# A fused attention and FFN block: phase 2 turns its rows on VectorE and places them through DRAM, gate logits in narrow tiles

## The chip, the cores and the metric

The kernel runs on one core of one Trainium2 chip. The core has TensorE (matrix products, written PE in the rows, its weight loads PEld), VectorE (DVE), ScalarE (ACT), GpSimd (POOL) and SyncE (SP), which issues all DMAs here; they move data between DRAM and the on-chip memories. TensorE writes to the accumulator memory PSUM only. Engines run side by side and wait for one another by semaphores; each takes its instructions in the order in which the program lists them. The metric is the device time of one execution in microseconds (us).

## What is computed

```python
def _L0_attn_ref(x, Wq, Wk, Wv, Wo, Wa, ba):
    q = _elu_plus_one((x @ Wq) ...)          # H = 16 heads of Dh = 64
    k = _elu_plus_one((x @ Wk) ...)
    v = (x @ Wv) ...
    a = jax.nn.sigmoid(x @ Wa + ba + DECAY_BIAS_SHIFT)
    def step(carry, inp):                    # over all tokens of a sequence
        S = at[..., None, None] * S + kt[..., :, None] * vt[..., None, :]
        z = at[..., None] * z + kt
        num = jnp.einsum('bhk,bhkv->bhv', qt, S)
        den = jnp.einsum('bhk,bhk->bh', qt, z) + eps
        return ((S, z), num / den[..., None])
    ...
    return out @ Wo

def _L0_ffn_ref(x, CB, SCB, bias):
    return jnp.einsum('bsk,nk->bsn', x, CB) * (SCB * (1.0 / 127.0)) + bias

x = L0_attn_x                                # (4, 2048, 512), float32
x = x + _L0_attn_ref(_layernorm(x), ...)
x = x + _L0_ffn_ref(_layernorm(x), ...)
```

## The kernel before

The 8192 tokens are cut into NC = 64 chunks of C = 128. The kernel has two phases, each a function per chunk that every engine runs in its own version; `steps` writes the first and last calls out and puts the middle ones, two chunks per turn, into a hardware loop. Products of full precision are made of three passes (`passes`): a number is split into a rounded high part and the rest, and high x high, high x low and low x high are added up in PSUM.

**Phase 1** (`step`, chunks -1 to NC + 1) makes q, k and v of a chunk from the normalised x (`unit`, `q_unit`, L1267), turns k, computes scores, the carried and the within-chunk part of the numerators and the state update, all as 64x64 tiles of the array. Once in two chunks (b == 1) `gate_logits` (L1395) makes the logits of the decay gates of the next two chunks: `wa` is padded to 64 columns, contraction rows are split in halves a, and the two chunks c lie in the output halves. The two halves a land in two PSUM banks, and VectorE adds them (`logit_sums`, L1049 and L1051). ScalarE makes the exponent, VectorE `decays` (L1057 to L1067): a reciprocal, a running product over each half chunk (two scans), and a zero at the head of each half. SyncE stores decays and products with four DMAs (`store_decays`), and when they have landed loads them back spread over partitions (`spread_decays`, `products`). The finished attention rows are turned by 32x32 blocks on VectorE (L1041) and stored as columns in DRAM (`attn_cols`, L415), so that phase 2 can load them already turned.

**Phase 2** (`step2`, chunks 1 to NC) does, for chunk i: TensorE multiplies the attention columns by Wo (`output_product`, 24 products of 128x512, in two halves of 12) into the bank Y. VectorE adds x (`residual`, L926: x1), takes statistics (L928), adds the bias to a copy (L933: x1b), GpSimd makes the reciprocal deviation (L627), VectorE the normalised rows (L941: x1n). TensorE turns these with eight small transposes (L1212, into the bank TF), ScalarE copies the high part (L842), VectorE subtracts (L1176), and TensorE does the FFN product of 12 passes (bank F). VectorE adds x1b (L1188: y) and SyncE stores y. The rows of the chunk after next are loaded by four DMAs for attention columns (`load_attn`, L427) and one for x (`load_x`, L433); their high and low parts are made by ScalarE (L696, `rows_hi`) and VectorE (L918, `rows_lo`).

TensorE's order in phase 2, at step i: first half of the output product of chunk i, the eight transposes of chunk i-1, second half of the output product, FFN product of chunk i-1:

```python
output_product(0, b, inputs_of_transposes)
...
turned = halves_turned([TF[:, a, :] for a in range(2)], j, x1n[1 - b])
...
output_product(1, b)
...
passes(F[1 - b], (fT_hi, fT_lo), (wf_hi, wf_lo), range(KT), KT).then_inc(F_ready, 1)
```

VectorE's order at step i: L1176 of i-1, `rows_lo` of i+1, `residual` of i with its statistics and normalisation, the output add of i-1. SyncE's: four loads and the x load of chunk i+1, the store of y of chunk i-2.

## Time and profile before

| | |
|---|---|
| median of 3 runs | 2018.64 us (2017.58 to 2019.59) |
| the profiled execution | 2018.3 us, of which the span from first to last instruction 2016.5 us |
| PE busy | 1989.3 us, 99% of the span |
| DVE busy | 1619.3 us, 80% |
| ACT busy | 684.3 us, 34% |
| POOL busy | 385.6 us, 19% |
| DMA | 220.62 MB, 109 GB/s in the mean |

Phase 1 ends at about 1430 us, phase 2 takes the rest. A line of a timeline gives start and length in us, the engine, the line of the code, the operation, what it writes <- what it reads, the tile of the array for products (rows*columns), the shape, and how many instructions were merged (x8); in square brackets the idle time before it and what ended that. SPq is the queue of SyncE: the length there is the time that issuing takes, not the transfer. Names are those of the buffers' owners: phase 2 reuses memory of phase 1, so x1 is shown as relu_t, x1b as exp_t, x1n as k, y as xt, and the high and low parts of everything as w_hi and w_lo. The timing of a product's end is modelled, so what counts is the distance from start to start.

### The profile page before, as it was taken

To read this page: it belongs to the slowest core of one execution; us is meant where nothing else is said; L and a number is where in the kernel's file an instruction comes from. 1 tells how busy PE (TensorE), PEld (TensorE's weight loads), DVE (VectorE), ACT (ScalarE), POOL (GpSimd) and SP (SyncE) were. 2 spreads that over 40 slices of the span, in tenths; PEclk is the share of its full clock that TensorE was granted. 3 is DMA by queue.
4 is the path that set the end of the run, shared out by engine and by line. 5 is a ranking of instruction groups with operands and counts; after the bars stand their busy time and mean duration, and the time that the engine had idled before them with its cause. 6 is when DMAs were issued, how large, how long until landed. Compare 5 with 4: busy or idle time off the path is not lost.

```text
span 2016.5 us, 69510 instructions
## 1 busy us (share of the span) xinstructions
PE 1989.3 (99%) x27422; PEld 1718.6 (85%) x27422; DVE 1619.3 (80%) x2918; ACT 684.3 (34%) x1288; POOL 385.6 (19%) x368
## 2 busy tenths in 40 slices
PE   8999999999999999999999999999899999999998
PEld 7888888888888888888888888888677777777776
DVE  8888888888888888888888888888856666566565
ACT  5333433443343344334334434434311111111111
POOL 3211223322222332212233212222100000000000
PEclk9999999999999999999999999999999999999999
DMA  6343434444343444334344433435544433434442
GB/s 211 86 95 95 113 96 106 106 103 94 95 113 96 107 104 104 94 95 113 96 107 105 103 94 95 115 95 121 135 122 125 116 116 122 125 114 117 123 123 81
DMA packets 461860, 220.62 MB, mean 109 GB/s; under 512 B 296832, under 2 KB 412032, under 8 KB 461824
## 3 DMA queue, kind: packets, MB, share of 16 engines
q1 hardware_dynamic: 461824, 220.15, 41.5%
q8 instruction: 22, 0.36, 0.1%
q14 instruction: 14, 0.11, 0.0%
HBM read 168.59 MB, written 51.44 MB: 109 GB/s over the span
## 4 chain that ended last, share of the span: by engine, by line
PE 95%; SPq 2%; issue 1%; DVE 1%; DMA 1%; POOL 0%; ACT 0%; POOLq 0%; DVEq 0%
PE G L1267 51%; PE DS L1224 18%; PE NUM L1224 9%; PE NUM L1336 3%; PE SC L1212 3%; PE SC L1389 3%; PE DS L1368 3%; PE NUM L1350 3%; PE DS L1409 1%; SPq L393 1%; SPq L415 0%; DMA abc<-decay_rows 0%; SPq L460 0%; SPq L469 0%; DMA norm_rows<-moments 0%
## 5 line engine op out<-in xcount | busy, mean ns | idle before, releaser
L1267 PE MATMUL G<-w_hi,xT_hi 128*128 128x512 f32 x1024 | 406.9, 397 | 0.9 <-DVE w_lo L880 0.9
L1267 PE MATMUL G<-w_lo,xT_hi 128*128 128x512 f32 x1024 | 399.6, 390 | 0.0
L1267 PE MATMUL G<-w_hi,xT_lo 128*128 128x512 f32 x1024 | 399.1, 390 | 0.0
L728 ACT ACTIVATE relu_t<-G 128x512 f32<-128x512 f32 x256 | 153.1, 598 | 445.7 <-PE G L1267 443.5
L1267 PE MATMUL G<-xT_hi,w_hi 128*128 128x256 f32 x1024 | 290.0, 283 | 0.0
L1267 PE MATMUL G<-xT_lo,w_hi 128*128 128x256 f32 x1024 | 289.8, 283 | 0.0
L1267 PE MATMUL G<-xT_hi,w_lo 128*128 128x256 f32 x1024 | 289.8, 283 | 0.0
L1267 PEld LDWEIGHTS G<-w_hi,xT_hi 128*128 128x128 f32 x1024 | 192.4, 188 | 41.8 <-DVE xT_lo L873 1.0
L1267 PEld LDWEIGHTS G<-w_hi,xT_lo 128*128 128x128 f32 x1024 | 192.2, 188 | 41.4
L1267 PEld LDWEIGHTS G<-w_lo,xT_hi 128*128 128x128 f32 x1024 | 192.6, 188 | 35.8
L1224 PE MATMUL DS<-w_hi 128*128 128x512 f32 x512 | 207.4, 405 | 2.6 <-DVE w_lo L918 2.3
L1224 PE MATMUL DS<-w_hi,w_lo 128*128 128x512 f32 x512 | 200.3, 391 | 0.0
L1224 PE MATMUL DS<-w_lo,w_hi 128*128 128x512 f32 x512 | 199.1, 389 | 0.0
L1267 PEld LDWEIGHTS G<-xT_hi,w_hi 128*128 128x128 f32 x1024 | 196.3, 192 | 3.3 <-DVE w_lo L880 0.4
L1267 PEld LDWEIGHTS G<-xT_hi,w_lo 128*128 128x128 f32 x1024 | 196.3, 192 | 2.4
L1267 PEld LDWEIGHTS G<-xT_lo,w_hi 128*128 128x128 f32 x1024 | 196.3, 192 | 0.0
L638 POOL TENSOR_TENSOR xT_in<-xT_in,bias_b 128x256 f32<-128x256 f32 x124 | 140.2, 1161 | 293.1 <-DMA bias_b<-norm_rows 293.1
L842 ACT ACTIVATE w_hi<-SC 128x512 fp32r<-128x512 f32 x64 | 38.2, 597 | 452.4 <-PE SC L1212 452.4
L642 POOL TENSOR_TENSOR xT_in<-xT_in,bias_b 128x256 f32<-128x256 f32 x124 | 177.6, 1463 | 2.4
L1074 DVE TENSOR_TENSOR_SCAN D<-abc,eye 128x512 f32<-128x512 f32 x128 | 175.7, 1372 | 1.9 <-DMA abc<-decay_rows 1.9
L623 POOL TENSOR_TENSOR moments<-vareps,minus_half 128x2 f32<-128x2 f32 x32 | 22.5, 702 | 731.8 <-DVE vareps L862 731.8
L1176 DVE TENSOR_TENSOR w_lo<-SC,w_hi 128x512 fp32r<-128x512 f32 x64 | 44.2, 691 | 140.2 <-ACT w_hi L842 140.2
(136 smaller groups left out, 3800.2 us busy)
## 6 DMA issues: line engine op xcount, KB each, us to landing
abc<-decay_rows SPq DMA_DIRECT2D x256, 128.0 KB, 3.0
pbc<-product_rows SPq DMA_DIRECT2D x256, 128.0 KB, 3.1
attn_cols<-attn SPq DMA_DIRECT2D x512, 64.0 KB, 2.2
at_rows<-attn_cols SPq DMA_DIRECT2D x256, 128.0 KB, 2.7
xt<-in_x SPq DMA_DIRECT2D x64, 256.0 KB, 3.1
x_in<-in_x SPq DMA_DIRECT2D x64, 256.0 KB, 3.1
out_rows<-xt SPq DMA_DIRECT2D x64, 256.0 KB, 3.0
xT_in<-in_xT SPq DMA_DIRECT2D x31, 512.0 KB, 4.3
```

Of the source, the lines that this page charges most:

```text
L638: made = pool.tensor_tensor(x4[:, kt, :, :], x4[:, kt, :, :], norm_b[:, 0, :, :], ALU.subtract)
L642: made = pool.tensor_tensor(x4[:, kt, :, :], x4[:, kt, :, :], norm_b[:, 1, :, :], ALU.mult)
L728: act.activation(relu_t[buffer][:, :], bank[:, :], ACT.Relu)
L1074: nc.vector.tensor_tensor_scan(D[:, hs(r), :].rearrange("p h c -> p (h c)"), abc[:, HH * L * r:HH * L * (r + 1)], eye8[:, :, :].rearrange( ...
L1176: nc.vector.tensor_tensor(by_stretch(fT_lo), both_of(TF), by_stretch(fT_hi).bitcast(fp32), ALU.subtract).then_inc(fT_lo_ready, 1)
L1212: turned.append(nc.tensor.transpose(to[a][:, L * j:L * j + L], rows[ps, 128 * j:128 * j + 128], ident[ps, ps]))
L1224: made = nc.tensor.matmul(to, a[:, kt, :], w[:, kt, :], start=(kt == 0 and n == 0), stop=(kt == tiles_k - 1 and n == 2))
L1267: made = nc.tensor.matmul(to, lhs, rhs, start=(n == 0), stop=(n == len(passes) - 1))
L1336: made = nc.tensor.matmul(num_of(a, e, j), qs[ps, GH * r + j, L * a:L * a + L], (S_mid if a else S[o])[ps, GH * r + j, :], start=(j == 0), ...
L1350: made = nc.tensor.matmul(num_of(a, e, j), M[ps, r, 2 * j + e, :], v1[o][ps, HH * r + 2 * j + e, :], start=False, stop=(j == GH - 1))
L1368: made = nc.tensor.matmul(DS[64 * e:64 * e + 64, U * a + E * j:U * a + E * j + E], k[ps, DH * h:DH * h + DH], vw[ps, h, :], start=True, st ...
L1389: made = nc.tensor.matmul(SC[64 * a:64 * a + 64, at:at + L], kT[ps, GH * r + j, ts], qT[ps, GH * r + j, C * (b ^ r) + L * a:C * (b ^ r) + ...
```

## The change

In phase 2 the eight transposes of TensorE go, except for the last chunk. In their place VectorE turns the normalised rows by 32x32 blocks (`x1t`), SyncE stores them with four DMAs into a scratch tensor in DRAM (`x1_cols`) so that the blocks come to lie where a full transposition would put them, and when these have landed loads the result with one DMA into `fT_in`; ScalarE and VectorE split that. The rows of the FFN weights are loaded in the matching order (16 DMAs instead of 4). The FFN product runs two chunks behind the output product instead of one, so TensorE's order at step i is: output product of i, FFN product of i-2. SyncE's order at step i is: stores of turned blocks of i-1, attention loads of i+2, x load of i+1, load of the placed blocks of i-1, store of y of i-3. VectorE's: normalised rows of i-1, their turning, low part of i-2, y of i-3, `rows_lo` of i+1, `residual` of i, the sum with bias of i-1, variance of i.

In phase 1 the gate logits are made with the full 128 contraction rows and 32 columns, in four column tiles, one for each chunk and half chunk, 64 tokens each, so no halves are added; everything behind them is 64 columns wide and not 128, the two scans become one, and the stores become five DMAs and not four. On TensorE the stage moves from ahead of the within-chunk product to behind it. At the seam of the phases some instructions are placed otherwise.

```diff
-        fT_hi, fT_lo = (w[:, 3, 2, :].rearrange("p (j c) -> p j c", c=C) for w in (w_hi, w_lo))
+        fT_hi, fT_lo = ([w[:, 3, 2 + b, :].rearrange("p (j c) -> p j c", c=C) for b in range(2)] for w in (w_hi, w_lo))
+        fT_in = [t.rearrange("p (j c) -> p j c", c=C) for t in pieces(kT, 2)]
+        x1t = pieces(D, 2)
...
-                    sp.dma_start(raw_wf[kt], CBT[128 * kt:128 * kt + 128, :]).then_inc(wf_loaded, 16)
+                    for x in range(4):
+                        at = 128 * x + SQ * kt
+                        sp.dma_start(raw_wf[kt][x:128:4, :], CBT[at:at + SQ, :]).then_inc(wf_loaded, 16)
...
                     for c in range(2):
                         n = chunk_at(i + 1 + c)
-                        sp.dma_start(decay_rows[bass.ds(n, 1), :].rearrange("o (a h t) -> (o h) a t", a=2, h=H),
-                                     aT[L * c:L * c + H, :].rearrange("h (a t) -> h a t", a=2)).then_inc(decay_stored, 16)
-                        sp.dma_start(product_rows[bass.ds(n, 1), :].rearrange("o (h c) -> (o h) c", h=H),
-                                     pT[L * c:L * c + H, :]).then_inc(decay_stored, 16)
-                    sp.wait_ge(decay_stored, p64[1])
+                        for a in range(2):
+                            g = GR * (2 * a + c)
+                            sp.dma_start(product_rows[bass.ds(n, 1), :].rearrange("o (h c) -> (o h) c", h=H)[:, L * a:L * a + L],
+                                         pT[g:g + H, :]).then_inc(decay_stored, 16)
+                    sp.wait_ge(decay_stored, p80[1])
...
+                turning = exists(i - 1) and exists(i)
+                if turning:
+                    sp.wait_ge(x1t_ready, one[-1])
+                    for g in range(4):
+                        q = SQ * g
+                        sp.dma_start(x1_cols[bass.ds(chunk_at(i - 1), 1), :]
+                                     .rearrange("o (f b t) -> (o f) b t", f=SQ, t=C)[:, :, q:q + SQ],
+                                     x1t[1 - b][q:q + SQ, :].rearrange("f (b t) -> f b t", t=SQ)).then_inc(x1t_stored, 16)
+                if exists(i + 2):
+                    sp.wait_ge(rows_loaded, r64[1])
                     for h in range(2):
-                        wait(sp, oT_lo_ready[h], one[-1])
-                    wait(sp, x1_ready, one[-1])
-                    load(chunk_at(i + 1), 1 - b)
-                if exists(i - 2):
-                    wait(sp, y_stored, y16[-3])
-                    wait(sp, y_ready, one[-2])
-                    sp.dma_start(out_rows[bass.ds(before, C), :], y[b]).then_inc(y_stored, 16)
-            steps(sp, step2, 1, NC + 2)
+                        sp.wait_ge(oT_lo_ready[h], one[0])
+                    load_attn(chunk_at(i + 2), b)
+                if exists(i + 1):
+                    sp.wait_ge(xin_loaded, x16[0])
+                    sp.wait_ge(x1_ready, one[-1])
+                    load_x(chunk_at(i + 1), 1 - b)
+                if turning:
+                    sp.wait_ge(x1t_stored, r64[-1])
+                    if isinstance(i, int) and i == 1:
+                        sp.wait_ge(scores_ready, NC + 1)
+                    if exists(i - 2):
+                        wait(sp, fT_loaded, x16[-2])
+                    if exists(i - 3):
+                        wait(sp, fT_lo_ready, one[-3])
+                    sp.dma_start(fT_in[1 - b].rearrange("p j c -> p (j c)"),
+                                 x1_cols[bass.ds(chunk_at(i - 1), 1), :].rearrange("o (p c) -> (o p) c", p=128))\
+                        .then_inc(fT_loaded, 16)
+                if exists(i - 3):
+                    wait(sp, y_stored, y16[-4])
+                    wait(sp, y_ready, counts(sp, i, 1, (-3,))[-3])
+                    sp.dma_start(out_rows[bass.ds(row(sp, i - 3), C), :], y[1 - b]).then_inc(y_stored, 16)
+            steps(sp, step2, 1, NC + 3)
             sp.wait_ge(y_stored, 16 * NC)
...
+                x16 = counts(act, i, 16, (-2,))
                 r64 = counts(act, i, 64, (1,))
-                act.wait_ge(fT_ready, one[-1])
-                act.activation(by_stretch(fT_hi), both_of(TF), ACT.Copy).then_inc(fT_hi_ready, 1)
+                if exists(i - 2):
+                    act.wait_ge(fT_loaded, x16[-2])
+                    if exists(i - 4):
+                        wait(act, F_ready, one[-4])
+                    act.activation(fT_hi[b], fT_in[b], ACT.Copy).then_inc(fT_hi_ready, 1)
...
-                dve.wait_ge(fT_hi_ready, one[-1])
-                nc.vector.tensor_tensor(by_stretch(fT_lo), both_of(TF), by_stretch(fT_hi).bitcast(fp32),
-                                        ALU.subtract).then_inc(fT_lo_ready, 1)
+                y16 = counts(dve, i, 16, (-4,))
+                r64 = counts(dve, i, 64, (-3,))
+                if isinstance(i, int) and i == NC:
+                    residual_normal(NC, x1[1 - b].rearrange("p (x j f) -> p x j f", x=4, f=SQ),
+                                    x1n[1 - b].rearrange("p (j f x) -> p x j f", x=4, f=SQ))
+                elif exists(i - 1):
+                    residual_normal(one[-1], x1[1 - b], x1n[1 - b])
+                if exists(i - 1) and exists(i):
+                    dve.wait_ge(x1n_ready, one[-1])
+                    if exists(i - 3):
+                        wait(dve, x1t_stored, r64[-3])
+                    nc.vector.transpose(x1t[1 - b], x1n[1 - b]).then_inc(x1t_ready, 1)
+                if exists(i - 2) and exists(i - 1):
...
+                if isinstance(i, int) and i == NC:
+                    dve.wait_ge(fT_hi_ready, NC)
+                    nc.vector.tensor_tensor(by_stretch(fT_lo[1 - b]), both_of(TF), by_stretch(fT_hi[1 - b]).bitcast(fp32),
+                                            ALU.subtract).then_inc(fT_lo_ready, 1)
+                if exists(i - 3):
...
-                        for c in range(2):
-                            for a in range(2):
-                                ps = slice(64 * a, 64 * a + 64)
-                                made = nc.tensor.matmul(DS[64 * c:64 * c + 64, U * a + ZC:U * a + 512], wa[ps, kt, :],
-                                                        xT_in[ps, kt, tokens(c)], start=(kt == 0), stop=(kt == KT - 1))
+                        for a in range(2):
+                            for c in range(2):
+                                g, t = GR * (2 * a + c), C * c + L * a
+                                made = nc.tensor.matmul(DS[g:g + GR, ZC:ZC + L], wa[:, kt, :], xT_in[:, kt, t:t + L],
+                                                        start=(kt == 0), stop=(kt == KT - 1))
...
                         pe.wait_ge(oT_lo_ready[h], one[0])
                     wait(pe, x1_ready, one[-2])
-                    if isinstance(i, int) and i == 1:
-                        output_product(0, b)
-                        output_product(1, b, inputs_of_transposes)
+                    for h in range(2):
+                        output_product(h, b)
+                if isinstance(i, int) and i == NC:
+                    pe.wait_ge(M_ready[1], NC)
+                    pe.wait_ge(x1n_ready, NC)
+                    for j in range(KT):
+                        turned = halves_turned([TF[:, a, :] for a in range(2)], j, x1n[1 - b])
+                    turned[1].then_inc(fT_ready, 1)
+                if isinstance(i, int) and i == 2:
+                    pe.wait_ge(wf_lo_ready, KT)
+                if exists(i - 2):
+                    if exists(i - 4):
+                        wait(pe, y_ready, one[-4])
                     else:
-                        output_product(0, b, inputs_of_transposes)
-                else:
-                    inputs_of_transposes()
-                for j in range(KT):
-                    turned = halves_turned([TF[:, a, :] for a in range(2)], j, x1n[1 - b])
-                turned[1].then_inc(fT_ready, 1)
-                if exists(i) and exists(i - 2):
-                    output_product(1, b)
-                if isinstance(i, int) and i == 1:
...
+                    pe.wait_ge(y_ready, NC - 2)
+                    ffn_product(NC, 1 - b)
             steps(pe, step2, 1, NC + 1)
```

## Rows read from the trace of the kernel before

**Rows 1.** The page: the chain that ended last, shares of the span by engine.
```profile
PE 95%; SPq 2%; issue 1%; DVE 1%; DMA 1%; POOL 0%; ACT 0%; POOLq 0%; DVEq 0%
```

**Rows 2.** Windows of phase 1 and phase 2. us, busy of PE, PEld, DVE, ACT, POOL; clock, DMA.
```profile
60.00:1380.00 1320.00, 1316.28 (x22986) 1176.38 (x22988) 1169.59 (x2086) 520.60 (x985) 327.82 (x270) 1.00 0.41 103
1500.00:1960.00 460.00, 460.00 (x2301) 366.43 (x2300) 282.03 (x524) 87.14 (x158) 28.07 (x52) 1.00 0.40 119
```

**Rows 3.** Timeline, one chunk of phase 2: start and duration in us, engine, line, operation.
```profile
1801.04 0.69 DVE L926 TENSOR_TENSOR relu_t<-DS,x_in 128x512 f32<-128x512 f32 x1 [0.34 <-PE DS L1224]
...
1804.11 0.55 DVE L941 TENSOR_SCALAR k<-relu_t,moments,rstd 128x512 f32<-128x512 f32 x1 [0.65 <-POOL rstd L627]
...
1806.05 0.39 PE L1224 MATMUL DS<-w_hi,w_lo 128*128 128x512 f32 x1
...
1806.76 0.19 PEld L1224 LDWEIGHTS DS<-w_hi 128*128 128x128 f32 x1
1806.76 0.50 PE L1224 MATMUL DS<-w_hi 128*128 128x512 f32 x1
...
1806.87 0.60 ACT L842 ACTIVATE w_hi<-SC 128x512 fp32r<-128x512 f32 x1 [6.98 <-PE SC L1212]
...
1807.50 0.69 DVE L1176 TENSOR_TENSOR w_lo<-SC,w_hi 128x512 fp32r<-128x512 f32 x1 [2.24 <-ACT w_hi L842]
...
1808.11 1.28 DVE L918 TENSOR_TENSOR w_lo<-at_rows,w_hi 128x512 fp32r<-128x512 f32 x2
...
1814.84 0.39 PE L1224 MATMUL DS<-w_hi,w_lo 128*128 128x512 f32 x1
```

**Rows 4.** Groups of VectorE: count | busy us, mean ns | idle before.
```profile
L1041 DVE STREAM_TRANSPOSE attn<-num_sb 128x512 f32<-128x512 f32 x128 | 91.1, 711 | 13.4 <-DMA attn_cols<-attn 0.2
...
L1060 DVE RECIPROCAL aT<-one_exp 128x128 f32<-128x128 f32 x32 | 30.5, 953 | 3.6 <-DVE one_exp L1057 0.5
```

**Rows 5.** Timeline of SyncE's DMA queue, phase 2.
```profile
1801.96 2.86 SPq L427 DMA_DIRECT2D at_rows<-attn_cols  x4
1805.02 0.43 SPq L433 DMA_DIRECT2D x_in<-in_x  x1
1805.68 0.36 SPq L592 DMA_DIRECT2D out_rows<-xt  x1
```

**Rows 6.** Timeline of SyncE's DMA queue, phase 1.
```profile
524.22 3.03 SPq L415 DMA_DIRECT2D attn_cols<-attn  x4
527.48 3.07 SPq L469 DMA_DIRECT2D pbc<-product_rows  x4
```

**Rows 7.** DMA issues: count, KB each, median us from issue to landing.
```profile
attn_cols<-attn SPq DMA_DIRECT2D x512, 64.0 KB, 2.2
...
x_in<-in_x SPq DMA_DIRECT2D x64, 256.0 KB, 3.1
```

**Rows 8.** Timeline, start and end of phase 2.
```profile
1475.68 0.69 DVE L926 TENSOR_TENSOR relu_t<-DS,x_in 128x512 f32<-128x512 f32 x1 [0.43 <-PE DS L1224]
...
2003.28 0.69 DVE L926 TENSOR_TENSOR relu_t<-DS,x_in 128x512 f32<-128x512 f32 x1 [1.64 <-PE DS L1224]
...
2010.11 0.62 PE L1224 MATMUL NUM<-w_hi,w_lo 128*128 128x512 f32 x1
```

**Rows 9.** Timeline of TensorE around the gate stage, phase 1.
```profile
537.55 0.71 PE L1212 MATMUL SC<-ident,k 64*128 64x64 f32 x16
538.19 0.27 PE L1336 MATMUL NUM<-S,qs 64*64 64x65 f32 x1
...
541.16 0.70 PE L1368 MATMUL DS<-vw,k 64*64 64x65 f32 x32
541.65 1.08 PE L1409 MATMUL DS<-xT_in,wa 64*64 64x128 f32 x32
542.52 0.67 PE L1350 MATMUL NUM<-v,M 64*64 64x65 f32 x32
```

**Rows 10.** Timeline of VectorE, the first reading of the gate logits.
```profile
544.33 0.28 DVE L1049 TENSOR_SCALAR logits<-DS 128x128 f32<-128x128 f32 x1
```

More of the change, by code:

```diff
@@ L573, in step2 @@
             def step2(i, _, b):
-                one = counts(sp, i, 1, (-2, -1))
-                x16 = counts(sp, i, 16, (0,))
-                r64 = counts(sp, i, 64, (0,))
-                y16 = counts(sp, i, 16, (-3,))
-                before = row(sp, i - 2)
-                if isinstance(i, int) and i == 2:
+                one = counts(sp, i, 1, (-3, -1, 0))
+                x16 = counts(sp, i, 16, (-2, 0))
+                r64 = counts(sp, i, 64, (-1, 1))
+                y16 = counts(sp, i, 16, (-4,))
@@ L894, in _ @@
             x_lo(1, 1, tiles_of(xT_bank(1)))
-            dve.wait_ge(small_loaded, 48)
+            dve.wait_ge(small_loaded, 80)
             nc.vector.tensor_scalar(wa[:, :, 0:H], wa_raw[:, :, :], 1.0, None, ALU.mult).then_inc(wa_ready, 1)
-            for c in range(2):
-                made = nc.vector.tensor_scalar(minus_ba[L * c:L * c + H, :], ba_c[L * c:L * c + H, :], -1.0, -SHIFT,
+            for g in range(0, 128, GR):
+                made = nc.vector.tensor_scalar(minus_ba[g:g + H, :], ba_c[g:g + H, :], -1.0, -SHIFT,
                                                ALU.mult, ALU.add)
@@ L928, in residual, with residual_deviation @@
                 nc.vector.bn_stats(stats2[:, :], x1[b]).then_inc(stats2_ready, 1)
-            def residual_rest(count, b):
+            def residual_deviation(count, biased=None):
                 dve.wait_ge(stats2_ready, count)
-                nc.vector.tensor_tensor(x1b[b], x1[b], bias_b[:, :], ALU.add)
+                if biased is not None:
+                    with_bias(biased)
                 nc.vector.bn_aggr(moments2[:, :], stats2[:, :]).then_inc(moments2_ready, 1)
@@ new lines, in step2 @@
+                if isinstance(i, int) and i == NC:
+                    dve.wait_ge(fT_hi_ready, NC)
+                    nc.vector.tensor_tensor(by_stretch(fT_lo[1 - b]), both_of(TF), by_stretch(fT_hi[1 - b]).bitcast(fp32),
+                                            ALU.subtract).then_inc(fT_lo_ready, 1)
+                if exists(i - 3):
+                    dve.wait_ge(F_ready, one[-3])
+                    dve.wait_ge(x1b_ready, one[-3])
+                    if exists(i - 4):
+                        wait(dve, y_stored, y16[-4])
+                    nc.vector.tensor_tensor(y[1 - b], F[1 - b], x1b[1 - b], ALU.add).then_inc(y_ready, 1)
@@ L1178, in step2 @@
+                if isinstance(i, int) and i == NC:
+                    dve.wait_ge(y_ready, NC - 2)
+                    with_bias(1 - b)
                 if exists(i + 1):
@@ L1181, in step2 @@
                     residual(one[0], x16[0], b)
-                if exists(i):
-                    residual_rest(one[0], b)
-                    residual_normal(one[0], b)
-                dve.wait_ge(F_ready, one[-1])
-                if exists(i - 3):
-                    wait(dve, y_stored, y16[-3])
-                nc.vector.tensor_tensor(y[1 - b], F[1 - b], x1b[1 - b], ALU.add).then_inc(y_ready, 1)
-            steps(dve, step2, 1, NC + 1)
+                    if isinstance(i, int) and i == 1:
+                        dve.wait_ge(bias_loaded, 16)
+                    residual_deviation(one[0], 1 - b)
+                if isinstance(i, int) and i == 1:
+                    ffn_weights_lo()
+            steps(dve, step2, 1, NC + 3)
         @block.tensor
```

147 lines of the change are left out of this document (70 added, 77 removed).

## The prediction

> **What bounds the kernel now.** I read the chain that ended last first: TensorE holds 95% of it [rows 1]. The reader is to see there that only what shortens TensorE's own list, or makes it wait, moves the time. The windows say the same of each stage: TensorE is busy for 1316.3 of 1320 us in phase 1 and for 460.0 of 460 in phase 2, while VectorE has 89% in the first and only 61% in the second [rows 2]. The clock is granted in full in both (1.00, the 2.4 GHz level). Next the timeline of one chunk of phase 2, to see what TensorE's 8.79 us are made of and how long each hand-over takes, then the DMA queue's own timeline, because the change puts a DRAM round trip in the middle of a chain that has none, and last the gate stage in phase 1.
>
> **Phase 2, the floor on TensorE.** From the last product ahead of one group of eight transposes to the same place a chunk later is 1814.84 - 1806.05 = 8.79 us. The step from that product to the first one behind the transposes is 0.71 us, and the next 35 steps take 1814.84 - 1806.76 = 8.08, so 0.231 each [rows 3]. The transposes thus cost 0.71 - 0.23 = 0.48 us a chunk. The change moves them to VectorE (only the last chunk keeps them). A chunk of TensorE's work becomes 36 x 0.231 = 8.31 us. If nothing else became late, 60 chunks would give 60 x 0.48 = 29 us. This is the gain that the change is after.
>
> **Phase 2, what is late next.** VectorE's work hides easily: it is 61% busy, and the new transposition costs 0.71 us if it is like that of the attention rows [rows 4], so it would stand at about 70%. What matters is the order on three queues that run strictly in order. Follow a chunk i from the start of its residual add, S(i).
> - VectorE and GpSimd: the normalised rows begin 1804.11 - 1801.04 = 3.07 after S(i) [rows 3]; the new step sits where VectorE waits for nothing in between, so this holds. They take 0.55, a tenth goes by to the dependent transposition, which takes 0.71. Turned blocks at S + 4.43.
> - SyncE starts a transfer 0.23 after the VectorE instruction that it waited for (1801.04 + 0.69 = 1801.73, the first load of the next rows is issued at 1801.96) [rows 3, 5]. First store at S + 4.66.
> - Now SyncE issues, in this order: four stores of turned blocks, four loads of attention columns, one load of x, and only then the load of the placed blocks. Four stores of the same shape (32 partitions, 512 runs of 128 bytes) occupy the queue for 527.48 - 524.22 = 3.26 [rows 6]. Four column loads take 1805.02 - 1801.96 = 3.06, the x load with the waits behind it 1805.68 - 1805.02 = 0.66 [rows 5]. For five more waits on semaphores that are already there I add 0.2. Sum 7.18: the load is issued at S + 11.84. The stores have landed by then (the last is issued at S + 7.1, median 2.2 to landing [rows 7]), so that wait is free.
> - The load is 256 KB in 2 KB runs like that of x, 3.1 to landing [rows 7]. S + 14.94.
> - ScalarE starts on it about 0.06 later; VectorE's subtraction starts 1807.50 - 1806.87 = 0.63 after ScalarE's copy [rows 3]. S + 15.63.
> - Behind this subtraction VectorE has, in order, the output add of an older chunk, two subtractions for attention rows, and the residual add of chunk i+2. Steps on that engine are 1808.11 - 1807.50 = 0.61 [rows 3], four of them with a few hundredths for waits 2.5. So S(i+2) = S(i) + 18.1.
>
> This is a ring that closes every two chunks: 18.1 / 2 = **9.05 us a chunk**, against 8.79 now and a floor of 8.31 on TensorE. The queue of SyncE itself needs 3.26 + 3.06 + 0.66 and about 1.4 for the placed load, the output store and the loop, 8.4 a chunk: below 9.05, but over TensorE's 8.31, so even a faster ring would not reach the floor. The products that wait for the subtraction (ready at S + 16.3) then let TensorE stand for about 0.75 us a chunk, perhaps 1.5 in every other one.
>
> Sixty chunks (residual adds at 1475.68 and 2003.28, 527.6 us, 8.79 each [rows 8]) become 30 x 18.1 = 543: **+15.4 us**. Bounds of the ring, from the same rows: transposition at 0.55 as the other 512-column instruction that reads one operand, queue steps at their shortest (0.72 instead of 0.79 and 0.76): 18.1 - 0.16 - 0.4 = 17.5, and a chunk is 8.75; landings half a microsecond later because the DMA engines, now 40% busy [rows 2], carry 512 KB more a chunk in part as 128-byte runs: 18.7, and a chunk is 9.35. I take the middle, since every term is a row of nearly the same instruction.
>
> The Trainium skill's page "VectorE: DVE Perf Modes", section "Rules for kernel authors", says to transpose 128x128 on TensorE where PSUM will do as the destination. By that rule the change goes the wrong way; by the floor alone it would be worth 29 us, by the ring it costs 15. No run so far shows which.
>
> **Start and end of phase 2.** At the start the residual add of chunk 1 no longer waits behind the FFN weights (four steps of 0.61, now a chunk later) and the first FFN product comes two chunks behind; following the queues as above brings the residual add of chunk 3 about 1 us earlier than 1475.68. **-1 us**, bounds -4 and +3. At the end the last residual add is now followed by 2016.5 - 2003.28 = 13.2 us. After the change chunk 62's placed blocks land at S(62) + 14.9, and S(63) is 8.4 to 9.1 behind S(62), so its product can start only at about S(63) + 7.5. Two FFN products of 12 steps stand behind it (5.5), then 0.4, the add 0.69 and the store 3.1: 17.2, **+4 us**. TensorE idles for over 3 us there; in the trace of before TensorE also idles between its last products, and the product at 2010.11 lasts 0.62 instead of 0.39 [rows 3, 8], which is the 1.2 GHz level. If all 24 run so, add 24 x 0.2 = 5. I take +6.
>
> **Phase 1, gate logits.** Once in two chunks, 31 times with this cost. Now 542.52 - 541.65 = 0.87 us for 32 pass records, in groups of four abreast: 8 groups x 0.109 [rows 9]. Each streams 128 columns; after the change 64, over 128 rows and 32 columns of the array. The stage before it streams 65 columns in 8 groups of four in 541.65 - 541.16 = 0.49, 0.06 each. If four tiles still run abreast: 8 x 0.06 = 0.47, a gain of 0.40. But the stage now stands between 64x64 tiles and the full array, one change of tiling more. Price: from the first transposes to the first product of the next tiling 538.19 - 537.55 = 0.64 go by [rows 9], of which eight steps of 0.06 are 0.48; the 0.16 left holds the start of a tiling and the change to the next. I take 0.14. Net 0.26 x 31 = **-8 us**.
> VectorE loses one of two instructions of 0.28 and half of a reciprocal of 0.95 [rows 4, 10], with the scan and the exponent about 1 us per pair. It is off the path by now, so this is worth nothing directly; it makes SyncE's decay stores earlier by as much, which pays for the fifth store (0.45). The logits are read at 544.33 [rows 10], and TensorE would deliver them at about 543 although the stage moved behind the within-chunk product (541.65 + 0.67 + 0.14 + 0.47 = 542.9): covered by over 1 us. Behind that read VectorE has the state update, which covers itself the same way.
>
> **Sum.** Profiled execution 2018.3 (span 2016.5; the median of the runs is 2018.6, the same within 0.02%). 2018.3 - 8 + 15.4 - 1 + 6 = 2030.7. I forecast **2031 us**.
>
> **The rivals.**
> - *The round trip fits* (faster). One mechanism: the load of placed blocks starts and lands so much sooner that the ring closes in less than twice 8.79. For it: 7.2 us of the ring are only issue time, and SyncE has idle time in phase 2 now. Against it: nothing in the issue order lets the load pass the nine transfers ahead of it. It decides below a ring of 17.6. Equality of the whole, with the other terms, lies at 17.7. At TensorE's floor: 2018.3 - 8 - 29 - 1 + 4 = **1984**; at SyncE's 8.4, **1990**. Chance 0.17 for anything faster by over 0.2% (a ring under 17.55).
> - *A draw*: a ring of 17.55 to 17.8, **2018**. 0.13.
> - *The gate tiles do not run four abreast.* Before has groups of four only with two row and two column halves; four column tiles need all rows for each. Two abreast makes 16 groups of 0.058, 0.93 us, dearer than now: 31 x 0.47 = 15 more than forecast, **2045**, 0.13. One at a time 32 x 0.058 = 1.86: **2074**, 0.03. The Trainium skill's page "TensorE: Matmul & The Clock Gate", Part 3, "The mechanism", holds that a weight load overlaps a running matmul only where the row group differs; by it the four would block one another. Against it: in the full array products step at 0.231 although a weight load lasts 0.19 and 512 columns at 2.4 GHz take 0.213 [rows 3], so there a load runs beside a product of the same rows; that is why I give it little.
> - *The ring is longer*: the fuller DMA queue lets loads land later. Landings 0.6 later make a ring of 18.7, 30 x 0.6 = 18 more, **2049**. 0.09.
> - Forecast (a ring of 17.8 to 18.5, four abreast) 0.45.
>
> A change within 0.2% (4 us) is what a measurement of this kernel can tell from none. Faster 0.17, same 0.13, slower 0.45 + 0.13 + 0.03 + 0.09 = 0.70. The range leaves out the faster end of the first rival and the 2074: 2008 to 2056. The likeliest case's own range is 2022 to 2042.
>
> **What would show it.** Right: in phase 2 ScalarE's copy of the placed blocks waits for a DMA, and VectorE and TensorE behind it; residual adds two chunks apart by 18.1 us; TensorE busy at about 92%, with gaps ahead of the FFN product and not ahead of the output product; SyncE's load of placed blocks issued 7.2 us behind the first store. In phase 1 the gate stage at 0.5 us and the step into it at 0.15. Wrong: a chunk of 8.3 to 8.5 in phase 2 with TensorE without gaps means that an issue or landing was priced too high; gate records stepping in pairs or singly mean the tiles block one another; a granted clock under 1 in the middle of phase 2 would be a cost that I have left out.

## The result and the profile after

The changed kernel takes 2025.24 us (median of 6, 2023.61 to 2031.62), the kernel before 2018.34 in the same comparison: a ratio of 1.0038, 95% interval 1.0024 to 1.0052. Its profiled execution took 2024.7 us, span 2022.9.

The chain that ended last, shares of the span by engine, in the page of the kernel after:

```profile
PE 66%; issue 24%; SPq 5%; DVE 2%; DMA 2%; POOL 1%; ACT 0%; POOLq 0%; DVEq 0%
```

Two windows of it, phase 1 and phase 2 (us, busy of PE, PEld, DVE, ACT, POOL; clock, DMA share, GB/s):

```profile
60.00:1380.00 1320.00, 1316.89 (x23052) 1172.85 (x23051) 1146.22 (x2041) 523.45 (x992) 334.38 (x270) 1.00 0.43 104
1500.00:1960.00 460.00, 433.61 (x1863) 346.32 (x1864) 310.93 (x572) 86.05 (x155) 28.12 (x52) 1.00 0.67 177
```

Against [rows 1, 2]: TensorE's part of the chain is down from 95% to 66%. The 24% of "issue" name no cause: in phase 2 the chain runs along GpSimd, whose long waits for VectorE's variance it doesn't follow further. The windows are the better reading here. Phase 1 is as full as before. In phase 2 TensorE now stands for 26 of 460 us, and the DMA share went from 0.40 to 0.67. The waits in the window of phase 2 name who holds it (engine, line, waited for: us, times, longest):

```profile
ACT w_hi L875 <- DMA kT<-x_cols: 368.0, 51, 8.3
DVE w_lo L1222 <- ACT w_hi L875: 110.0, 52, 3.2
...
PE NUM L1279 <- DVE w_lo L1222: 25.8, 36, 1.5
```

All of TensorE's 26 us are waits for the subtraction behind the placed load. They are spread over 36 of 52 chunks. One round in the timelines of VectorE, ScalarE and SyncE's queue:

```profile
1796.05 0.68 DVE L963 TENSOR_TENSOR relu_t<-DS,x_in 128x512 f32<-128x512 f32 x1
...
1805.47 0.68 DVE L963 TENSOR_TENSOR relu_t<-DS,x_in 128x512 f32<-128x512 f32 x1
...
1808.54 0.55 DVE L983 TENSOR_SCALAR k<-relu_t,moments,rstd 128x512 f32<-128x512 f32 x1 [0.65 <-POOL rstd L655]
1809.12 0.71 DVE L1219 STREAM_TRANSPOSE D<-k 128x512 f32<-128x512 f32 x1
1811.14 0.69 DVE L1222 TENSOR_TENSOR w_lo<-kT,w_hi 128x512 fp32r<-128x512 f32 x1 [1.31 <-ACT w_hi L875]
...
1813.56 0.68 DVE L963 TENSOR_TENSOR relu_t<-DS,x_in 128x512 f32<-128x512 f32 x1
```

```profile
1810.48 0.63 ACT L875 ACTIVATE w_hi<-kT 128x512 fp32r<-128x512 f32 x1 [6.41 <-DMA kT<-x_cols]
```

```profile
1800.60 3.02 SPq L594 DMA_DIRECT2D x_cols<-D  x4
1803.87 2.84 SPq L436 DMA_DIRECT2D at_rows<-attn_cols  x4
1806.96 0.38 SPq L442 DMA_DIRECT2D x_in<-in_x  x1
1807.52 0.34 SPq L614 DMA_DIRECT2D kT<-x_cols  x1
1808.11 0.36 SPq L620 DMA_DIRECT2D out_rows<-xt  x1
1810.00 3.02 SPq L594 DMA_DIRECT2D x_cols<-D  x4
```

The reader is to see a residual add at 1796.05, the first store of its turned blocks 4.55 us later, the placed load (L614) 6.92 behind that store, ScalarE starting on it 2.96 later, VectorE 0.66 after that, and the residual add two chunks on 2.42 after VectorE: 17.51 us in all. The residual add, the turning and the stores at 1805.47, 1809.12 and 1810.00 are those of the chunk between. That is the ring of the prediction, link for link.

The difference of the spans, 6.4 us, splits at three marks that every trace has: the last product into the bank G (the end of the q, k and v products of phase 1), the residual add of chunk 3, that of chunk 63. Chunks are counted from 0 here and in the prediction, so chunk 63 is the last and is made in step 64 of the code. The "seam" is the time between the first two marks, the "tail" what follows the third. In the kernel after:

```profile
1423.81 0.39 PE L1321 MATMUL G<-w_hi,xT_lo 128*128 128x512 f32 x1
...
1475.29 0.69 DVE L963 TENSOR_TENSOR relu_t<-DS,x_in 128x512 f32<-128x512 f32 x1 [1.38 <-PE DS L1279]
...
2005.88 0.69 DVE L963 TENSOR_TENSOR relu_t<-DS,x_in 128x512 f32<-128x512 f32 x1 [0.93 <-PE DS L1279]
```

In the kernel before the first of them is this, the other two are [rows 8]:

```profile
1432.20 0.39 PE L1267 MATMUL G<-w_hi,xT_lo 128*128 128x512 f32 x1
```

So phase 1 gained 8.4 us, the seam between the phases went from 43.5 to 51.5 (+8.0), the 60 chunks from 8.79 to 8.84 each (+3.0), the tail from 13.2 to 17.1 (+3.8). The first mark moves by itself from one execution to the next: in the twelve kernels below whose phase 1 has the gate part it lies between 1419.3 and 1425.8, so phase 1's share of one comparison is known to some 3 us.

### The profile page after: what moved, and what is told of

Same layout as the page of the kernel before. It is cut to its first block, busy times and chain, and to the rows that moved or that the text cites. A ratio compares the mean times of both kernels' runs of the same rounds, so it can differ in the third digit from the quotient of the medians.

```text
span 2022.9 us, 69690 instructions
## 1 busy us (share of the span) xinstructions
PE 1954.3 (97%) x26918; PEld 1688.2 (83%) x26918; DVE 1624.5 (80%) x2919; ACT 684.2 (34%) x1288; POOL 390.7 (19%) x368
## 4 chain that ended last, share of the span: by engine, by line
PE 66%; issue 24%; SPq 5%; DVE 2%; DMA 2%; POOL 1%; ACT 0%; POOLq 0%; DVEq 0%
PE G L1321 50%; PE NUM L1390 3%; PE SC L1443 3%; PE DS L1422 3%; PE NUM L1404 3%; PE SC L1269 2%; SPq L424 1%; POOL rstd L655 1%; PE DS L1463 1%; SPq L400 1%; DMA kT<-x_cols 1%; SPq L436 1%; SPq L412 1%; SPq L594 0%; SPq L470 0%
## 5 line engine op out<-in xcount | busy, mean ns | idle before, releaser
L1279 PE MATMUL DS<-w_hi 128*128 128x512 f32 x512 | 200.3, 391 | 12.2 <-DVE w_lo L955 12.2
L666 POOL TENSOR_TENSOR xT_in<-xT_in,bias_b 128x256 f32<-128x256 f32 x124 | 140.0, 1160 | 298.2 <-DMA bias_b<-norm_rows 298.2
L875 ACT ACTIVATE w_hi<-kT 128x512 fp32r<-128x512 f32 x63 | 39.8, 632 | 459.7 <-DMA kT<-x_cols 459.7
L670 POOL TENSOR_TENSOR xT_in<-xT_in,bias_b 128x256 f32<-128x256 f32 x124 | 183.9, 1514 | 2.4
L757 ACT ACTIVATE exp_t<-G 128x512 f32<-128x512 f32 x256 | 151.8, 593 | 0.0
```

The source lines that it names most:

```text
L666: made = pool.tensor_tensor(x4[:, kt, :, :], x4[:, kt, :, :], norm_b[:, 0, :, :], ALU.subtract)
L670: made = pool.tensor_tensor(x4[:, kt, :, :], x4[:, kt, :, :], norm_b[:, 1, :, :], ALU.mult)
L757: act.activation(exp_t[buffer][:, :], bank[:, :], ACT.Exp).then_inc(ready, 1)
L1279: made = nc.tensor.matmul(to, a[:, kt, :], w[:, kt, :], start=(kt == 0 and n == 0), stop=(kt == tiles_k - 1 and n == 2))
```

## The experiments

Each ratio is against the kernel before on the same chip, with its 95% interval. The columns are cut out of the traces by the marks above, in us. "Ring" is the mean distance of residual adds two chunks apart (chunks 5 to 59); "issue" is the time from the first store of turned blocks to the issue of the placed load, "landing" from that issue to ScalarE's start on it.

| kernel | last into G | seam | a chunk | tail | ring | issue | landing | ratio |
|---|---|---|---|---|---|---|---|---|
| before | 1432.2 | 43.5 | 8.79 | 13.2 | | | | 1 |
| after | 1423.8 | 51.5 | 8.84 | 17.1 | 17.77 | 6.90 | 3.21 | 1.0038 |
| gates_only | 1422.6 | 43.5 | 8.79 | 11.8 | | | | 0.9952 (0.9939 to 0.9965) |
| phase2_only | 1429.9 | 50.6 | 8.82 | 17.4 | 17.72 | 6.90 | 3.14 | 1.0078 (1.0064 to 1.0091) |
| wf_four | 1424.9 | 42.9 | 8.93 | 17.0 | 17.88 | 6.92 | 3.23 | 1.0014 (1.0004 to 1.0024) |
| load_early | 1421.3 | 48.9 | 8.61 | 17.5 | 17.23 | 4.72 | 3.73 | 0.9950 (0.9938 to 0.9962) |
| load_late | 1425.8 | 48.8 | 9.42 | 16.6 | 18.88 | 7.52 | 3.68 | 1.0178 (1.0165 to 1.0191) |
| y_act | 1422.7 | 50.7 | 9.03 | 17.5 | 18.13 | 6.89 | 3.62 | 1.0079 (1.0065 to 1.0092) |
| early_y | 1423.7 | 42.4 | 8.53 | 17.5 | 17.04 | 5.26 | 3.49 | 0.9879 (0.9863 to 0.9894) |
| both_act | 1422.3 | 43.4 | 8.34 | 17.8 | 16.72 | 4.85 | 3.94 | 0.9828 (0.9815 to 0.9841) |
| both_w16 | 1422.9 | 49.6 | 8.25 | 15.1 | 16.55 | 4.77 | 3.81 | 0.9845 (0.9829 to 0.9861) |
| both_yfirst | 1423.8 | 43.2 | 8.51 | 17.9 | 17.10 | 5.14 | 4.33 | 0.9913 (0.9899 to 0.9927) |
| both_fill | 1421.1 | 44.8 | 8.29 | 15.5 | 16.61 | 4.82 | 3.77 | 0.9807 (0.9792 to 0.9821) |
| both_all | 1419.3 | 45.5 | 8.58 | 16.2 | 17.21 | 5.25 | 4.31 | 0.9908 (0.9893 to 0.9923) |

**The two parts, each alone.** gates_only is the kernel before with the gate part of the diff, phase2_only the kernel after without it.

> The kernel before with the gate part of the change alone: 128x32 weight tiles, gate products behind the within-chunk products, phase 2 as it was. My theory (phase 1 gains 0.27 us a pair of chunks, and nothing of it is given back): the last product into G ends 8.4 us earlier than in the kernel before, as in the trace of the changed kernel, the seam stays at 43.5 us and a chunk of phase 2 at 8.79, so the time is 2018.3 - 8.4 = 2010. Rival (what phase 1 gains is handed back at the seam, where transfers or the clock set the end): the last product into G earlier by 8, the seam longer by as much, 2018.

> The changed kernel with the gate part of the change undone, and phase 2 as the change has it. Theory A (the two parts add): the kernel before, plus 8 us at the seam, 3 to 6 us over the 60 chunks, 4 in the tail: 1.0075 to 1.009 of the kernel before, 2033 to 2036. Rival B (the seam is late only because phase 1 ends earlier than SyncE's queue can follow): the seam shorter than 51.5 us by some of the 8.4, and 1.004 to 1.006.

Both of my theories held: -0.48% and +0.78%, in the sum +0.30%, where the whole change has +0.38 (0.24 to 0.52). The gate part gives 9.6 us by the first mark (1422.6 against 1432.2), where 8.4 was forecast, and nothing of it is handed back: the seam stays at 43.5. All of the loss is phase 2, with a seam of 50.6 in phase2_only too. That kernel's first mark lies 2.3 us ahead of the one before without any gate part, which is within the scatter of the mark. The gate stage itself, timeline of TensorE in the kernel after:

```profile
538.98 0.68 PE L1404 MATMUL NUM<-v,M 64*64 64x65 f32 x32
539.59 0.65 PE L1463 MATMUL DS<-xT_in,wa 128*32 128x64 f32 x32
540.17 0.50 PE L1321 MATMUL G<-w_hi,xT_hi 128*128 128x512 f32 x1
```

32 products of 128x32 tiles take 540.17 - 539.59 = 0.58 with the change of tiling behind them, where 0.47 + 0.14 was forecast [rows 9]. In the trace the products start in fours, from one four to the next 0.056, and each change of tiling takes 0.15 where a step within the stage takes 0.056. So the four column tiles do run abreast.

**The seam.** wf_four loads each of the four FFN weight tiles by one DMA.

```diff
-                    for x in range(4):
-                        at = 128 * x + SQ * kt
-                        sp.dma_start(raw_wf[kt][x:128:4, :], CBT[at:at + SQ, :]).then_inc(wf_loaded, 16)
+                    sp.dma_start(raw_wf[kt], CBT.rearrange("(x k f) n -> k f x n", x=4, f=SQ)[kt])\
+                        .then_inc(wf_loaded, 16)
```

> The changed kernel, but each of the four FFN weight tiles is loaded by one DMA (the same permuted rows) and not by four. Theory A (SyncE's 12.6 us of issuing for the 16 loads makes the seam late: the attention stores and the weight tiles queue behind it): SyncE spends under 4 us on the weight loads, the seam (last product into G to the residual add of chunk 3) falls from 51.5 to 43 to 46 us, and the time to 2017 to 2020. Rival B (the seam is long because the first trips through DRAM start the two-chunk ring late): seam 50 to 52, time 2024 to 2026.

SyncE's queue at the seam, first the kernel after:

```profile
1426.48 6.42 SPq L412 DMA_DIRECT2D abc<-in_CBT  x8
1432.94 6.20 SPq L412 DMA_DIRECT2D qT<-in_CBT  x8
1439.19 0.58 SPq L414 DMA_DIRECT2D bias_b<-in_bias  x1
1439.81 2.65 SPq L424 DMA_DIRECT2D attn_cols<-attn  x4
```

then wf_four:

```profile
1427.87 1.23 SPq L410 DMA_DIRECT2D abc<-in_CBT  x2
1429.14 1.25 SPq L410 DMA_DIRECT2D qT<-in_CBT  x2
1430.44 0.59 SPq L413 DMA_DIRECT2D bias_b<-in_bias  x1
1431.07 3.77 SPq L423 DMA_DIRECT2D attn_cols<-attn  x4
```

and the weight loads of the kernel before:

```profile
1434.12 1.71 SPq L403 DMA_DIRECT2D abc<-in_CBT  x2
1435.87 0.91 SPq L403 DMA_DIRECT2D qT<-in_CBT  x2
```

Issuing takes 12.6 us in the kernel after, 2.5 in wf_four and 2.6 in the kernel before, and the attention stores behind it go out 8.7 us sooner in wf_four than in the kernel after. In the kernel after VectorE and TensorE stand for them (waits from 1424 to 1475, then the timeline):

```profile
PE DS L1279 <- DVE w_lo L955: 12.2, 1, 12.2
DVE attn L1083 <- DMA attn_cols<-attn: 10.5, 2, 8.0
```

```profile
1444.36 0.71 DVE L1083 STREAM_TRANSPOSE attn<-num_sb 128x512 f32<-128x512 f32 x1 [8.04 <-DMA attn_cols<-attn]
1455.04 0.76 PE L1279 MATMUL DS<-w_hi 128*128 128x512 f32 x1 [12.19 <-DVE w_lo L955]
```

In wf_four the same two waits are 6.0 and 1.4 us, and the granted clock is at the 1.2 GHz level for 6.8 us at the seam (from 1447.4), not for 17 (from 1445.5 and from 1466.0, the first time while TensorE stood for 12.2 us, the second after it had stood for 2.5). Theory A holds for the seam: 51.5 becomes 42.9. The time fell by less, 0.24% or 5 us, and misses the forecast of 2017 to 2020; in the profiled execution the 60 chunks came out longer (8.93 each, 5.5 us in all), and why is not shown. A second pair, further down, tests the seam again.

**The ring or the queue.** load_early and load_late move only the place of the placed load in SyncE's order.

```diff
 # load_early: stores of i-1, then
+    load_x(i + 1); load_attn(i + 2), first of four
+    wait for the stores; load of placed blocks
+    load_attn(i + 2), other three
 # load_late: the store of y ahead of the load of placed blocks
```

> The changed kernel, but in phase 2 SyncE issues, behind the four stores of turned blocks, the x load, one attention load, then waits for the stores and issues the load of placed blocks, and then the other three attention loads: the same DMAs in another order. Theory A (a ring over two chunks through SyncE's issues sets the period of 8.84 us): the ring loses some 2 us of its 17.7, so 15.7 / 2 = 7.9 falls under TensorE's 8.16, and the period becomes 8.2 to 8.4; time 2025 - 60 x 0.45 to 0.64 = 1987 to 1998. Rival B (the number of SyncE's issues, or traffic, sets the period, not their order): 8.8 as before, 2025.

> The changed kernel, but the load of placed blocks is issued behind the store of y, not ahead of it. Theory A (ring over two chunks): the ring grows by the one issue, 0.6 us, so the period by 0.3 us: 8.84 to 9.14, time 2025 + 18 = 2043. Rival B (SyncE's number of issues or TensorE sets the period): no change, 2025.

The order moves the time both ways, so the number of issues alone (rival B of both) is out. load_late: the issue part grows by 0.62 and the landing by 0.47, and the ring by 1.11, which is their sum: 0.58 a chunk, 28 us by the ratios. The mechanism was as forecast, the size nearly twice it, since the landing was taken as fixed, and TensorE idles enough for its clock to fall now and then (0.98 in the window). load_early: 2.2 less of issue, but the period only falls to 8.61, where theory A had 8.2 to 8.4. Here another wait is last. VectorE's part behind the subtraction, 2.41 in the kernel after, is 3.38. What fills the 0.97 is a wait of VectorE ahead of the output add for the landing of an earlier store of y, the last DMA of SyncE's round (window 1500 to 1960):

```profile
DVE xt L1237 <- DMA out_rows<-xt: 46.0, 53, 1.6
```

The kernel after has no such wait. And SyncE's queue, which in the kernel after waits for VectorE 39 times, hardly ever waits (window 1500 to 1960, first after, then load_early):

```profile
SPq L594 <- DVE D L1219: 27.3, 39, 1.7
```

```profile
SPq L596 <- DVE D L1223: 2.3, 9, 0.5
```

A full round of its queue in load_early, with nothing between the DMAs that the profile shows as a wait:

```profile
1795.73 3.02 SPq L596 DMA_DIRECT2D x_cols<-D  x4
1799.01 0.40 SPq L444 DMA_DIRECT2D x_in<-in_x  x1
1799.65 0.61 SPq L438 DMA_DIRECT2D at_rows<-attn_cols  x1
1800.44 0.46 SPq L616 DMA_DIRECT2D kT<-x_cols  x1
1801.10 2.04 SPq L438 DMA_DIRECT2D at_rows<-attn_cols  x3
1803.39 0.38 SPq L624 DMA_DIRECT2D out_rows<-xt  x1
1804.49 3.03 SPq L596 DMA_DIRECT2D x_cols<-D  x4
```

Eleven DMAs take the queue 8.76 us here and 8.62 in the mean (8.39 to 9.09), which is the period. So the ring sets the period of the changed kernel, and SyncE's issuing is next, 0.2 us below it.

**Off SyncE's queue.** y_act gives the store of y to ScalarE's queue. both_act gives it the load of placed blocks too, and has the four weight DMAs. early_y is load_early with the y store on ScalarE and the four weight DMAs.

```diff
 # ScalarE, step2, behind rows_hi of chunk i+1
 ...
+    act.wait_ge(x1t_stored, r64[-1])
+    act.dma_start(fT_in[1 - b]..., x1_cols[chunk i-1]).then_inc(fT_loaded, 16)   # both_act
 ...
+    wait(act, y_ready, one[-3])
+    act.dma_start(out_rows[row of i-3], y[1 - b]).then_inc(y_stored, 16)         # y_act, both_act, early_y
```

> The changed kernel, but the store of y is issued by ScalarE's queue, behind its hi parts of the attention rows, and not by SyncE: SyncE issues nine DMAs a chunk, not ten. Theory A (the two-chunk ring of 17.77 us sets the period; the store of y isn't on it): period 8.8 to 8.9, time as the changed kernel's, 0.38% above the kernel before. Rival B (SyncE's issuing, 8.3 us a chunk and 0.5 of waiting, sets the period): it falls by the 0.6 to 0.7 us of the store, to 8.2, so -36 us, 1.5% under the kernel before.

> The changed kernel with the FFN weight tiles in four DMAs, and in phase 2 both the load of placed blocks and the store of y issued by ScalarE behind its hi parts of the attention rows. The ring is then 4.36 + 0.22 + 2.44 (four stores) + 2.15 (landing) + 0.1 + 3.2 to 3.7 (landing of the load) + 0.66 + 2.41 = 15.5 to 16.0 us, 7.8 to 8.0 a chunk, SyncE 7.3: both under TensorE's 8.16. Theory A (ring, then SyncE, then TensorE in that order of price): period 8.2 to 8.3, 60 chunks x 0.55 to 0.65 = -33 to -39, the seam -5: 1.2 to 1.8% under the kernel before, 1982 to 1995. Rival B (DMA traffic bounds phase 2: landings grow as the period shrinks): period over 8.6, 0.6% or less under the kernel before, 2006 or more.

> The changed kernel with the FFN weight tiles in four DMAs, the load of placed blocks issued early by SyncE (as in load_early) and the store of y issued by ScalarE. In load_early the ring had 1 us of slack (17.23 with 3.38 behind the lo part, where 2.41 is the least) and SyncE waited for nothing: if SyncE's issuing set its 8.61 us a chunk (theory A), one DMA less gives 8.0, and the ring (16.3 / 2 = 8.15) or TensorE (8.16) comes next: 8.2 to 8.3, 1.2 to 1.8% under the kernel before. Rival B (the landing of the placed load, which grew from 3.2 to 3.7 us in load_early, grows again and the ring bounds): 8.5 to 8.6, 0.5 to 0.7% under.

y_act settles ring against queue: SyncE has a DMA less (ten a chunk and not eleven; the expectation counts one too few on both sides) and waits 68.1 us instead of 27.3 in the window, and the kernel is no faster but slower: the landing on the ring went from 3.21 to 3.62 and the ring from 17.77 to 18.13. both_act is the test of the whole account: a chunk at 8.34, just above the 8.2 to 8.3 of theory A, and 1.7% under the kernel before, inside its 1.2 to 1.8%. The ring is 16.7 and not 15.5 to 16.0: the landing is 3.94 and not 3.2 to 3.7, the issue part 4.85 and not 4.69, and the part behind the subtraction 2.70 and not 2.41. TensorE is busy for 454.8 of 460 us there. ScalarE now waits for another landing as well, that of the attention rows, and passes a part of it on to VectorE behind the subtraction (10.1 us in the window):

```profile
ACT w_hi L717 <- DMA at_rows<-attn_cols: 39.4, 44, 1.4
```

In early_y my numbers of theory A did not come. Its 8.53 is rival B's number, not rival B's reason: the landing of the load did not grow (3.49 against 3.73 in load_early), while SyncE waited for the stores' landing, which rose from 2.2 to 2.8 for the last of the four:

```profile
SPq L614 <- DMA x_cols<-D: 25.4, 43, 1.2
```

That wait lies on the ring: the issue part is 5.26, where load_early has 4.72. Of its 0.7% against load_early, up to 6.5 us (0.3%) are the shorter seam of the four weight DMAs. Which wait bounds the 8.53 was not isolated.

**Seam again, the landing, the tail.** All three start from both_act: sixteen weight DMAs again; the y store ahead of the placed load; fourteen products into an unused bank in the two gaps of the tail. both_all has the last two.

```diff
 # both_fill, TensorE, step 64
+                    filling(6)          # nc.tensor.matmul(G[0], oT_hi[1][:, 0, :], wo_hi[:, 0, :]), six times
                     pe.wait_ge(x1n_ready, NC)
                     ... eight transposes
+                    filling(8)
```

> both_act with the FFN weight tiles in sixteen DMAs again, as the change has them; nothing else differs. Theory A (SyncE's issuing of the sixteen makes the seam late, whatever the period behind it): the seam (last product into G to the residual add of chunk 3) goes from 43.4 back to 50 to 52 us, and the time from 0.9828 of the kernel before to 0.986 to 0.987 (7 to 8 us). Rival B (the seam isn't on the path once the ring is short): the same time as both_act.

> both_act with ScalarE's store of y ahead of the load of placed blocks, not behind it. In the runs so far the landing of that load took 3.2 us where no store of y was issued within 0.6 us of it (the changed kernel) and 3.6 to 3.9 where one was issued just ahead of it or overlapped it (load_late 3.7, y_act 3.6, both_act 3.9). Theory A (packets of the store of y delay it): the store is now issued 1 to 2 us sooner, the landing falls to 3.2 to 3.5, the ring of 16.7 by 0.4, the period from 8.34 to 8.2: -8 us, 1976. Rival B (the attention loads beside it set its landing, not the y store): landing 3.8 to 4.0, the same time as both_act.

> both_act with fourteen products whose result nobody reads (six ahead of the last chunk's transposes, eight behind them) in TensorE's two idle stretches of the tail. Theory A (the clock at half costs the tail its time: 13 products at 0.427 us, where 0.227 is the full clock's): the clock stays at full, the tail from the last residual add falls from 17.8 to 15.0 to 15.5, 2.5 us in all. Rival B (the fills delay the transposes and the last products as much as the clock gives): 17.5 to 18.5.

> both_yfirst and both_fill together. If both theories A hold, 1984 - 8 - 2.5 = 1973 to 1975, 0.977 to 0.979 of the kernel before; if only one does, its share.

both_w16: the seam is 49.6 against 43.4, so it belongs to the weight DMAs in a second pair. The time rises by 0.17%, some 3 us, with overlapping intervals, and not by 7 to 8: the 60 chunks and the tail of the profiled execution were shorter by 5 and 3 us. That a shorter seam is worth less than its length shows in both pairs; what takes the rest is open.

both_yfirst: neither theory's number. The landing rose to 4.33 and the kernel lost 0.85%. ScalarE waits there for y, and so in 23 of 54 chunks its store goes out less than 1.5 us ahead of the placed load (1807.52 and 1808.37 in one chunk), in the others up to 4.0 us ahead (1815.52 and 1818.34 in the next). The two kinds differ: the load lands in 4.84 us where the store is that close ahead of it, and in 3.93 where it is further. So a store of y close ahead goes with a later landing, as theory A supposed; but with the store further ahead the landing is only that of both_act, and the 3.2 to 3.5 of theory A did not come.

both_fill: theory A. The last FFN products, TensorE, first both_act:

```profile
1972.88 0.63 PE L1285 MATMUL NUM<-w_lo,w_hi 128*128 128x512 f32 x1
1973.30 0.63 PE L1285 MATMUL NUM<-w_hi,w_lo 128*128 128x512 f32 x1
```

then both_fill:

```profile
1968.02 2.11 PE L1566 MATMUL G<-w_hi 128*128 128x512 f32 x8
1969.96 0.39 PE L1285 MATMUL NUM<-w_hi 128*128 128x512 f32 x1
1970.19 0.39 PE L1285 MATMUL NUM<-w_lo,w_hi 128*128 128x512 f32 x1
```

The step is 0.23 and not 0.43, the clock stays at the 2.4 GHz level, and the tail is 15.5 against 17.8. both_w16 had a tail of 15.1 without fills, in an execution whose clock did not fall either. Of the twelve profiled executions without fills the clock fell in the tail of ten, of the two with fills in none, so the fill seems to make certain what sometimes happens. The intervals of the two kernels (0.9807 and 0.9828) overlap, so a gain in the time is not shown.

both_all: 0.9908, where 0.977 to 0.979 was forecast if both held. It has the late landing of both_yfirst (4.31), and its clock does not fall in the tail (16.2 against 17.9).

The fastest kernel found is both_fill at 0.9807, 39 us under the kernel before and 47 under the changed one by the ratios.

## Why the prediction was right, and where it was not

The forecast was 2031 us, slower by 0.6%; it is slower by 0.38%, inside the range and inside the likeliest case's own range. Term by term, measured against forecast: phase 1 -8.4 (-8), the 60 chunks +3.0 (+15.4), the seam +8.0 (-1), the tail +3.8 (+6); sum +6.4 (+12.4). Two of the four are good, two are wrong with opposite signs, and that the sum is so near is in part luck: with the 60 chunks as measured and the seam as forecast it would have been 2018, a draw, the other way round 2040. The signs that were named came: ScalarE waits for the placed load, VectorE and TensorE behind it, the gaps lie ahead of the FFN product, and TensorE is busy at 94% in phase 2, where 92% was forecast.

- **The floor on TensorE** is right and a little lower: without transposes a step is 0.2266, so 36 make 8.16, not 8.31. No kernel reached it; both_w16 came to 8.25.
- **The ring** is right as a mechanism, and its price was too high. From the residual add, measured (forecast): turned blocks 4.36 (4.43), first store 0.22 (0.23), issue part 6.90 (7.18), landing with ScalarE's start 3.21 (3.16), to VectorE 0.66 (0.63), to the residual add two chunks on 2.41 (2.5): 17.77 for 18.1. The mis-sized term is the issue part: the four stores took 3.27 as forecast, the loads 3.09, but the x load with the waits 0.56 where I had 0.66 and another 0.2 for five waits. The waits on semaphores that are already there hardly lengthened the gaps between DMAs: 0.25, 0.25 and 0.18 in the round shown above, 0.20 and 0.23 in [rows 5]. A third of a microsecond in the ring is 10 us over 30 rounds; the other 2.5 us of the 12.4 between +15.4 and +3.0 are the last round, which took 15.05 (1990.83 to 2005.88) and not 17.8.
- **The start of phase 2**, forecast at -1 with bounds -4 and +3, is the failed step. I followed the queues of chunks 0 to 3 and moved the FFN weights' subtraction, but the diff's sixteen weight loads stand in front of the attention stores on SyncE, and their twelve extra issues I priced at nothing. The sixteen take 12.6 us of the queue at 0.79 each, the four of the kernel before 2.6: 10 us more. The seam came out at +8.0, and with four loads (wf_four, and both_act against both_w16) it is back at 42.9 and 43.4.
- **The tail** was right in kind: +3.8 for +6, with products at 0.43 at the half level for seven steps only and not for 24.
- **The gates**: right (-8.4 for -8, the stage with the change behind it 0.58 for 0.61), and the rival that the tiles block one another is out: 32 weight loads of 0.11 and 32 products take 0.58 us together. The page "TensorE: Matmul & The Clock Gate" of the Trainium skill, Part 3, "The mechanism", says that a weight load overlaps a running matmul only where the row group differs. The four tiles here share all rows, so this trace does not agree.
- **SyncE's queue** at 8.4 was a little too low: with the ring shortened (load_early) it is 8.6 and sets the period.
- **The rival that the round trip fits** was priced at 1984 and 1990 us. It did not come with this order, but it was priced rightly: with the load and the store of y off SyncE's queue and four weight loads the same trip through DRAM runs at 8.34 a chunk and 1984.4 us (both_act). The Trainium skill's page "VectorE: DVE Perf Modes", "Rules for kernel authors", would leave the 128x128 transposes to TensorE. The runs agree for the change as written (phase2_only, +0.78%) and not for the version with the shorter ring (both_act, -1.72% against -0.48% for the gate part alone).
- The longer ring through later landings was a rival at 0.09 and did not come in the changed kernel (3.21). Later landings did come in the kernels with another order or queue for the placed load or the store of y (3.5 to 4.3).

## What to carry to other kernels

Where work is moved off the engine that bounds, follow one item from its start to the point where its result releases the next item of its kind, issue times of in-order queues included: that ring, divided by the items in flight, is the least that the new period can be, and so is each queue's own sum of issues (8.6 us here, when the ring was shorter). Of a step that is moved behind a DMA, ask first which DMA issues stand ahead of it on its queue, and whether another engine's queue is idle at that moment. Count every DMA of a diff, also those that run once: in these traces each occupies the issuing queue for 0.34 to 0.8 us, and at the seam that was on the path.

## What the runs showed of the hardware that was not expected

- The landing of the same 256 KB load ranged in the mean from 3.2 to 4.3 us with what was issued around it: 3.21 with attention and x loads ahead and the y store 0.6 us behind, 3.6 to 3.7 in load_early, load_late and y_act, 3.9 in both_act, and in both_yfirst 4.84 with the y store less than 1.5 us ahead of it and 3.93 with more. The bytes under way beside it do not explain the order: by the packets that start between its issue and its landing y_act has some 500 KB beside it, the kernel after 630. The rule is open.
- A DMA over 128 partitions with rows gathered in fours took SyncE 0.62 us to issue (wf_four, 256 KB), one over 32 partitions at a stride of four 0.79 (the kernel after, 64 KB). The bytes do not set it: in load_early's round shown above the stores of 64 KB took 0.76 each, the x load of 256 KB 0.40.
- Column tiles of 128x32 run four abreast, though they share all rows: 32 products of 64 columns in 0.58 us with the change of tiling.
